# Chosen tokens' rows moved by indirect DMA instead of one-hot products, in an attention layer with a routed feed-forward

## The chip, the cores and the metric

The kernel runs on one core of a Trainium2 chip. The metric is the device time of one execution in microseconds. The profile and the trace are those of one execution; times in it count from its first instruction.

## What is computed

x has 8 batches of 512 tokens with 512 features, all fp32. Two layers follow each other, each with a residual sum:

```
x = x + attention(layernorm(x), Wq, Wk, Wv, Wg, Wo)      # 16 heads of 128, three kinds of attention, gated
z = layernorm(x);  w = z @ W_r + b_r                       # one routing weight a token
top 128 tokens by w are looked at; a token is chosen if w > the 128th value   (127 of 512 a batch)
x = x + (gelu(z[chosen] @ W1 + b1) @ W2 + b2) * w[chosen]  # chosen tokens; 2048 hidden features
x = x + z                                                  # the others
```

The change concerns the second layer only. It has a routing part, which finds each batch's chosen tokens and packs their rows of z into 128 slots (one stays empty), and an experts' part, two dense products over 8 x 128 slots, whose result goes back to the tokens' own rows.

## The kernel before

Up to about 1816 us of the trace the attention layer is computed; the change doesn't touch it. It leaves the heads' output in DRAM (o_scratch).

**Precision.** A product in fp32 is made from three fp32r products: each operand is split in a high half (a rounded copy, made by ScalarE) and a low half (value minus high half, by VectorE or GpSimd), and high times high, high times low and low times high are added in one bank.

**project_and_route (L1019).** For each batch the heads' output is multiplied by Wo. The 16 heads come in K = 4 chunks of G = 4. A chunk of batch b+1 is loaded by SyncE (load_o, 1 MB) into one of two raw buffers, ScalarE makes the high half (high, L1129), GpSimd the low half (chunks.low, L1015), and TensorE multiplies (chunk, L1191): 48 matmuls for all four blocks of 128 tokens. The routing of batch b is placed between the chunks of batch b+1, in an order written out by hand: in `body(b)` TensorE runs chunk 0 and chunk 1, then one product that spreads the routing weights as a row (L1210), chunk 2, two tiny products that give each chosen token its slot (L1218, L1219), half of chunk 3, then the packing (L1227 and L1231), then the other half of chunk 3.

VectorE adds x and the product (x1, L1264), takes mean and variance, makes z2 (L1288), the weights (L1295), counts how many weights are at least each token's (L1308), marks chosen tokens (sel), adds z of those not chosen (L1325), makes onehot (L1333: token against slot) and adds b2 times the weight (L1339). x1 is then the base of the output and SyncE stores it in base_scratch (L1108). As x1 is one buffer, L1264 of the next batch waits until this store has landed (base_stored), and row block t of the next batch's chunk 0 waits until L1264 has read bank t.

Packing a batch: 16 fp32 products of z2 with onehot (L1227, 32 passes in the trace) give z of the 128 slots, transposed; ScalarE and VectorE split it into zsel_hi and zsel_lo (L1149, L1342). Four transposes of onehot (L1231) give `place`, kept for later.

SyncE issues all transfers from one queue, in the order of its program. In `body(b)`: chunk 1 of batch b+1, x of batch b+1, chunk 2, chunk 3, chunk 0 of batch b+2, each behind the wait that frees its buffer, then the store of x1. At the start of the stage `load_first` (L995, L998) loads Wo's chunks and the first batch's chunks through the two raw buffers; the next Wo chunk waits until VectorE has made the low half of the one before (chunks.low_wo, L1010). Four small loads follow the first pair (L1113 to L1116).

**experts (L1354).** Two groups of 4 batches, 16 steps each, one per 128 hidden features. A step is `hidden` (L1551, 12 matmuls of the packed z with W1) for the step after, then 12 matmuls (L1589) of gelu's result with W2, accumulated in banks 0 to 3. The weights come by SyncE (L1424, L1425), their low halves by GpSimd (L1486). The first six steps of group 0 run inside the last batch's routing, where TensorE has no chunks left.

When a group is done its four banks are split (L1524, L1622) and `spread` (L1564, two matmuls for each of 4 blocks a batch) multiplies them by `place`, which puts the 128 slots back on 512 rows. VectorE multiplies by the weight and adds base (L1630); base comes back from DRAM (load_base, L1434) and goes to the output (L1439). For group 0 this happens one block a step during group 1, for group 1 at the end.

The loops over batches and over the steps of group 0 are loops of the engines (Fori).

## Time and profile before

| what | value |
|---|---|
| time, 3 runs | 2433.12, 2435.80, 2437.37 us; median 2435.8 |
| the profiled execution's own time | 2433.43 us |
| its span, first to last instruction | 2431.6 us |
| TensorE, VectorE, ScalarE, GpSimd busy | 2350.1, 1913.1, 1521.4, 1588.7 us |
| mean granted TensorE clock | 0.991 of 2.4 GHz |
| routing and projection | about 1816 to 2209 us |
| last batch's routing with the first expert steps | 2209 to 2262 us |
| experts after it | 2262 to 2431.6 us |

A row of the chain of waits has the start and the length of a piece, both in us, and the engine and line that worked or was waited for; it goes back from the last instruction through whatever released each step. A timeline row has the same two numbers, an instruction with its shapes and count, and in square brackets the idle time before it with what ended it. PE is TensorE, DVE VectorE, ACT ScalarE, POOL GpSimd, SPq the queue of SyncE.

### The profile page before, as it was taken

What the parts mean: (1) busy time and instruction counts of PE and PEld (TensorE: products, weight loads), DVE (VectorE), ACT (ScalarE), POOL (GpSimd) and SP (SyncE); (2) the same over time, 40 slices, a digit from 0 to 9 for tenths busy, and PEclk for the clock granted to TensorE, in tenths of its full rate; (3) what the DMA queues carried; (4) which work ended last, traced back from release to release, by engine and by line L of the source; (5) the groups of instructions that cost most, each with busy time, mean ns of one, the idle gap of its engine ahead of it and who ended that gap; (6) DMA issues with size and microseconds to landing.
All of it is one profiled execution on the core that took longest, in us unless ns stands there. A gap on an engine that the chain in (4) does not pass through costs nothing. (4 is left out here: it accounts for less than half of the span.)

```text
span 2431.6 us, 42771 instructions
## 1 busy us (share of the span) xinstructions
PE 2350.1 (97%) x13456; PEld 2067.5 (85%) x13456; DVE 1913.1 (79%) x6101; ACT 1521.4 (63%) x4192; POOL 1588.7 (65%) x1206
## 2 busy tenths in 40 slices
PE   6899999999999999999999999999969999999998
PEld 5799899989888998998999898889967888887776
DVE  7489898988888898988889888889864777775223
ACT  7577777777777777777777777777753222213442
POOL 1677877787787778778777877877744333433442
PEclk9999999999999999999999999999989999999999
DMA  5212222232222222222212222222225334332266
GB/s 169 73 53 66 72 75 62 66 83 55 66 72 75 54 74 78 60 62 76 75 53 75 76 62 60 78 56 63 62 99 187 121 103 154 139 104 87 97 184 221
DMA packets 143214, 215.44 MB, mean 89 GB/s; under 512 B 15136, under 2 KB 53408, under 8 KB 141984
## 3 DMA queue, kind: packets, MB, share of 16 engines
q1 hardware_dynamic: 143008, 212.95, 29.5%
q8 instruction: 99, 1.62, 0.3%
q14 instruction: 107, 0.88, 0.1%
HBM read 94.66 MB, written 51.12 MB: 60 GB/s over the span
## 5 line engine op out<-in xcount | busy, mean ns | idle before, releaser
L555 POOL TENSOR_TENSOR s_full<-s_full,rope 128x512 f32<-128x512 f32 x256 | 334.8, 1308 | 340.3 <-DMA s_swap<-s_full 340.0
L559 POOL TENSOR_TENSOR s_full<-s_full,s_swap 128x512 f32<-128x512 f32 x256 | 331.3, 1294 | 36.7
L556 POOL TENSOR_TENSOR s_swap<-s_swap,rope 128x512 f32<-128x512 f32 x256 | 331.2, 1294 | 0.0
L563 POOL TENSOR_TENSOR qk_lo<-s_full,qk_hi 128x512 fp32r<-128x512 f32 x256 | 326.5, 1296 | 0.0
L718 ACT ACTIVATE pt_hi<-bank 128x384 fp32r<-128x384 f32 (+1 forms) x384 | 174.9, 528 | 221.4 <-PE bank L657 221.0
L1015 POOL TENSOR_TENSOR o_lo<-o_raw,o_hi 128x2048 fp32r<-128x2048 f32 x32 | 149.6, 4675 | 241.7 <-ACT o_hi L1129 202.1
L613 PE MATMUL bank<-wv_hi,xt_hi 128*128 128x256 f32 x1024 | 300.2, 293 | 0.0
L724 ACT ACTIVATE bank<-bank,shift 128x512 f32<-128x512 f32 (+3 forms) x512 | 256.7, 501 | 58.9 <-DVE bank L829 58.3
L613 PE MATMUL bank<-wv_hi,xt_lo 128*128 128x256 f32 x1024 | 289.9, 283 | 0.0
L613 PE MATMUL bank<-wv_lo,xt_hi 128*128 128x256 f32 x1024 | 289.8, 283 | 0.0
L829 DVE TENSOR_REDUCE bank<-bank 128x8 f32<-128x512 f32 (+3 forms) x512 | 253.1, 494 | 0.0
L825 DVE TENSOR_REDUCE shift<-bank 128x1 f32<-128x512 f32 (+3 forms) x512 | 246.4, 481 | 0.0
L847 DVE SCALAR_TENSOR_TENSOR bank<-bank,coef,cb 128x192 f32<-128x192 f32 (+1 forms) x512 | 195.5, 405 | 50.4 <-ACT probs L743 50.3
L730 ACT ACTIVATE win<-win,shift 128x192 f32<-128x192 f32 (+1 forms) x512 | 225.5, 440 | 0.0
L713 ACT ACTIVATE qk_hi<-s_full 128x512 fp32r<-128x512 f32 x256 | 161.3, 630 | 83.5 <-POOL s_full L559 78.7
L600 PE MATMUL bank<-xt_hi,wq_hi 128*128 128x512 f32 x512 | 208.5, 407 | 3.4 <-PEq L193 3.4
L1191 PE MATMUL bank<-wo_hi,o_hi 128*128 128x512 f32 x512 | 204.6, 400 | 5.8 <-PEq L463 3.3
L839 DVE TENSOR_TENSOR pt_lo<-bank,pt_hi 128x384 fp32r<-128x384 f32 (+1 forms) x384 | 207.0, 595 | 1.1 <-ACT pt_hi L718 1.1
L600 PE MATMUL bank<-xt_hi,wq_lo 128*128 128x512 f32 x512 | 200.9, 392 | 0.0
L1191 PE MATMUL bank<-wo_hi,o_lo 128*128 128x512 f32 x512 | 200.0, 391 | 0.0
L1191 PE MATMUL bank<-wo_lo,o_hi 128*128 128x512 f32 x512 | 199.8, 390 | 0.0
L600 PE MATMUL bank<-xt_lo,wq_hi 128*128 128x512 f32 x512 | 199.4, 389 | 0.0
(181 smaller groups left out, 7028.3 us busy)
## 6 DMA issues: line engine op xcount, KB each, us to landing
s_swap<-s_full SPq DMA_DIRECT2D x512, 128.0 KB, 2.3
o_scratch<-s_swap SPq DMA_DIRECT2D x128, 256.0 KB, 2.0
o_raw<-o_scratch SPq DMA_DIRECT2D x32, 1024.0 KB, 6.2
w_raw<-in_L_ffn_W SPq DMA_DIRECT2D x64, 256.0 KB, 3.0
xin<-in_L_attn_x SPq DMA_DIRECT2D x14, 1024.0 KB, 5.6
base_scratch<-x SPq DMA_DIRECT2D x8, 1024.0 KB, 4.7
base<-base_scratch SPq DMA_DIRECT2D x32, 256.0 KB, 4.3
out<-base SPq DMA_DIRECT2D x32, 256.0 KB, 3.6
```

The lines of the kernel that those rows point to most:

```text
L555: nc.gpsimd.tensor_tensor(s_full[k][:], s_full[k][:], rope[:, 0, :], ALU.mult).then_inc(cos_done[k], 1)
L556: nc.gpsimd.tensor_tensor(s_swap[k][:], s_swap[k][:], rope[:, 1, :], ALU.mult).then_inc(sin_done[k], 1)
L559: nc.gpsimd.tensor_tensor(s_full[k][:], s_full[k][:], s_swap[k][:], ALU.add).then_inc(roped[k], 1)
L563: nc.gpsimd.tensor_tensor(qk_lo[k][:], s_full[k][:], f32(qk_hi[k][:]), ALU.subtract).then_inc(lo_done[k], 1)
L600: last = nc.tensor.matmul(banks[QK_BANK[k]][:, :], w[k][s][:, c, :], v[:, b, c, :], start=(n == 0), stop=(n == 3 * C - 1))
L613: last = nc.tensor.matmul(out, x[:, b, c, at:at + P], w[:, c, :], start=(n == 0), stop=(n == 3 * C - 1), skip_group_check=True)
L724: nc.scalar.activation(n, n, ACT.Exp, bias=shift1[:, t:t + 1], scale=-1.0, accum_out=sums[:, 1, t:t + 1]).then_inc(exp_row, 1)
L730: nc.scalar.activation(win[:, t, lo:], win[:, t, lo:], ACT.Exp, bias=shift2[:, t:t + 1], scale=-1.0, accum_out=sums[:, 2, t:t + 1]).then_i ...
L825: nc.vector.tensor_reduce(shift1[:, t:t + 1], n[:, 0:(t + 1) * P], AX.X, ALU.min)
L829: nc.vector.reduce_sum(sc[:, t, 0:nb], n[:, 0:nb * BS].rearrange("p (n s) -> p n s", s=BS), AX.X).then_inc(row_read, 1)
L839: nc.vector.tensor_tensor(pt_lo[:, PTOFF[g]:PTOFF[g] + w], banks[PT_BANK[g]][:, 0:w], f32(pt_hi[:, PTOFF[g]:PTOFF[g] + w]), ALU.subtract). ...
L1191: last = nc.tensor.matmul(banks[t][:, :], o[k % 2][:, g, t * P:(t + 1) * P], w[:, k * G + g, :], start=(k == 0 and n == 0), stop=(k == K - ...
```

## The change

Routing no longer packs rows by products. `store_z` writes z2 of a batch to DRAM (1 MB, rows of 2 KB); four tiny products of onehot with `tags` (a token's number and weight) give each slot its token (`info`); GpSimd turns that into row addresses and fetches the 128 rows by indirect DMA (`fetch_z`); in the next batch TensorE transposes them (`turn_rows`, four transposes) and ScalarE and VectorE split them (`z_high`, `z_low`). x1 is stored straight in the output, by rows of 2 KB. In the experts' part `fetch` gets the 128 rows of a batch from the output by indirect DMA, `final` adds the result times the weight in one instruction a batch, and `put_back` writes them to the output by indirect DMA; `place`, `spread`, the split of the results, load_base and store are gone. For the last batch the packing lies in group 0 behind step 11 (TURN). The loops over batches, over GpSimd's chunks and over group 0's steps are written out.

```diff
+    late = np.concatenate([before, slot, ones, p[:, None] - FAR], 1)
...
+    z_rows = r("z_rows", [P, D])
+    row_at, away = r("row_at", [P, B, 2], mybir.dt.int32), r("away", [P, B, 2])
+    z_dram = [nc.dram_tensor(f"z_scratch{b}", [N, D], F32, kind="Internal").ap() for b in range(B)]
+    tags = r("tags", [P, T, 2])
     G, K, wo_hi, wo_lo = chunks.G, chunks.K, chunks.wo_hi, chunks.wo_lo
...
         eng.wait_ge(chunk_used, B * K + 1)
+    def fetch_z(pool, b):
+        pool.wait_ge(info_done, b + 1)
+        for i, start in enumerate((0, b * N)):
+            nc.gpsimd.tensor_scalar(away[:, b, i:i + 1], info[:, b, 0:1], float(FAR + start), None, ALU.add).then_inc(rows_addressed, 1)
+        pool.wait_ge(rows_addressed, 3 * b + 2)
+        nc.gpsimd.tensor_copy(row_at[:, b], away[:, b]).then_inc(rows_addressed, 1)
+        pool.wait_ge(rows_addressed, 3 * b + 3)
+        pool.wait_ge(z2_stored, 16 * (b + 1))
+        if b:
+            pool.wait_ge(zsel_ready, b)
+        nc.gpsimd.indirect_dma_start(z_rows[:], None, z_dram[b], bass.IndirectOffsetOnAxis(ap=row_at[:, b, 0:1], axis=0),
+                                     bounds_check=N - 1, oob_is_err=False).then_inc(z_rows_loaded, 16)
+    def turn_rows(pe, b):
+        pe.wait_ge(z_rows_loaded, 16 * (b + 1))
+        if b:
+            pe.wait_ge(zsel_lo_done, b)
+        for c in range(C):
+            last = nc.tensor.transpose(banks[7][:, c * P:(c + 1) * P], z_rows[:, c * P:(c + 1) * P], m("ident"))
+        last.then_inc(zsel_ready, 1)
+    def z_high(act, b):
+        act.wait_ge(zsel_ready, b + 1)
+        nc.scalar.activation(zsel_hi[:, :, b * P:(b + 1) * P], banks[7][:, :].rearrange("p (c s) -> p c s", c=C), ACT.Copy)\
+            .then_inc(zsel_hi_done, 1)
+    def z_low(dve, b):
+        dve.wait_ge(zsel_hi_done, b + 1)
+        nc.vector.tensor_tensor(zsel_lo[:, :, b * P:(b + 1) * P], banks[7][:, :].rearrange("p (c s) -> p c s", c=C),
+                                f32(zsel_hi[:, :, b * P:(b + 1) * P]), ALU.subtract).then_inc(zsel_lo_done, 1)
     ex_sync, ex_gpsimd, ex_scalar, ex_tensor, ex_vector = experts(
-        nc, at, chunks, r, banks, zsel_hi, zsel_lo, place, weight, base_dram,
-        (wait_used, wait_raw_free, wait_split_free, zsel_lo_done, place_done, base_stored), w1, b1, w2, b2, out)
+        nc, at, chunks, r, banks, zsel_hi, zsel_lo, info, row_at, (fetch_z, turn_rows, z_high, z_low),
...
+            def store_z(b):
+                sp.wait_ge(z2_ready, b * T + T)
...
                 if more:
                         load_o(b + 1, k)
                         if k == 1:
                             load_x(b + 1)
+                            store_z(b)
                     if more != "next":
                         load_o(b + 2, 0)
                 else:
                     for f in range(EARLY + 2):
                         first(f)
+                        if f == 3:
+                            store_z(b)
                 sp.wait_ge(base_ready, b * T + T)
-                sp.dma_start(base_dram[bass.ds(b, 1)].rearrange("o p t d -> p (o t) d"), x1[:]).then_inc(base_stored, 16)
+                sp.dma_start(out[b].rearrange("(t p) d -> p t d", p=P), x1[:]).then_inc(base_stored, 16)
...
                 act.wait_ge(step, b * NS + 9)
                 nc.scalar.activation(sd[:], ve[:], ACT.Sqrt).then_inc(sd_ready, 1)
+                if b:
+                    z_high(act, b - 1)
...
-                act.wait_ge(zsel_ready, b + 1)
-                nc.scalar.activation(zsel_hi[:, :, bass.ds(b * P, P)], banks[6][:, :].rearrange("p (c s) -> p c s", c=C),
-                                     ACT.Copy).then_inc(zsel_hi_done, 1)
-                act.wait_ge(place_ready, b + 1)
-                nc.scalar.activation(place[:, bass.ds(b, 1), :], banks[7][:, :], ACT.Copy).then_inc(place_done, 1)
+                act.wait_ge(info_ready, b + 1)
+                nc.scalar.activation(info[:, b, :], banks[6][:, 0:2], ACT.Copy).then_inc(info_done, 1)
...
                 chunks.low(pool, 0, k, 1)
-            with pool.Fori(0, B - 1) as b:
-                for k in range(K):
+            nc.gpsimd.memset(z_rows[:], 0.0).then_inc(rows_cleared, 1)
+            pool.wait_ge(rows_cleared, 1)
+            chunks.low(pool, 1, 0, 0)
+            for b in range(B - 1):
+                for k in range(1, K):
                     chunks.low(pool, b + 1, k, k % 2)
+                if b < B - 2:
+                    chunks.low(pool, b + 2, 0, 0)
+                fetch_z(pool, b)
             first, rest = ex_gpsimd(pool)
...
                 if more:
                     chunk(b + 1, 0)
+                    if b:
+                        turn_rows(pe, b - 1)
...
                 else:
                     first(5)
                 pe.wait_ge(onehot_ready, b * T + T)
-                for c in range(C):
-                    for t in range(T):
-                        last = nc.tensor.matmul(banks[6][:, c * P:(c + 1) * P], z2[:, t, c * P:(c + 1) * P], onehot[:, t, :],
-                                                start=(t == 0), stop=(t == T - 1))
-                last.then_inc(zsel_ready, 1)
                 for t in range(T):
-                    last = nc.tensor.transpose(banks[7][:, t * P:(t + 1) * P], onehot[:, t, :], m("ident"))
-                last.then_inc(place_ready, 1)
+                    last = nc.tensor.matmul(banks[6][:, 0:2], onehot[:, t, :], tags[:, t, :], start=(t == 0), stop=(t == T - 1))
+                last.then_inc(info_ready, 1)
...
                 after()
+                if b:
+                    dve.wait_ge(z2_stored, 16 * b)
                 for t in range(T):
...
-                did(v.tensor_scalar(weight[:, bass.ds(b, 1), :], wraw[:].rearrange("p (o t) -> p o t", o=1), br_all[:, 0:1], None, ALU.add))
+                if b:
+                    dve.wait_ge(info_done, b)
+                else:
+                    dve.wait_ge(tags_set, 1 + T)
+                did(v.tensor_scalar(tags[:, :, 1], wraw[:], br_all[:, 0:1], None, ALU.add))
                 after()
                 for t in range(T):
                     v.tensor_scalar(diag[:, t * P:(t + 1) * P], m("ident"), wcol[:, t:t + 1], None, ALU.mult).then_inc(diag_ready, 1)
+                if b:
+                    z_low(dve, b - 1)
                 if not more:
                     first(2)
                 dve.wait_ge(row_ready, b + 1)
...
-                dve.wait_ge(zsel_hi_done, b + 1)
-                v.tensor_tensor(zsel_lo[:, :, bass.ds(b * P, P)], banks[6][:, :].rearrange("p (c s) -> p c s", c=C),
-                                f32(zsel_hi[:, :, bass.ds(b * P, P)]), ALU.subtract).then_inc(zsel_lo_done, 1)
                 assert at[0] == NS, (at[0], NS)
             v.memset(selcum[:], 0.0)
+            v.memset(tags[:], 0.0).then_inc(tags_set, 1)
+            dve.wait_ge(tags_set, 1)
+            dve.wait_ge(small_loaded, 64)
+            for t in range(T):
+                v.tensor_scalar(tags[:, t, 0:1], number, float(t * P), None, ALU.add).then_inc(tags_set, 1)
             for k in range(1, K):
                 chunks.low_wo(dve, k)
             first, rest = ex_vector(dve)
...
-        if g:
-            for f in range(FT):
-                body(g * FT // 2 + f // 2, f % 2, f, f == 0, f == FT - 1)
-            return
-        with eng.Fori(begun // 2, FT // 2 - 1) as pair:
-            for s in range(2):
-                body(pair, s, pair * 2 + s, False, False)
-        for s in range(2):
-            body(FT // 2 - 1, s, FT - 2 + s, False, s == 1)
+        for f in range(0 if g else begun, FT):
+            body(g * FT // 2 + f // 2, f % 2, f, f == 0, f == FT - 1)
...
+            tiles(sp, 1, load)
+            sp.wait_ge(base_stored, 16 * (B + 1))
+            sp.wait_ge(rows_stored, 16 * B)
...
+        def fetch(b):
+            pool.wait_ge(rows_cleared, 1)
+            pool.wait_ge(base_stored, 16 * (b + 2))
+            nc.gpsimd.indirect_dma_start(rows[:, b, :], None, out_rows, bass.IndirectOffsetOnAxis(ap=row_at[:, b, 1:2], axis=0),
+                                         bounds_check=B * N - 1, oob_is_err=False).then_inc(rows_loaded[b], 16)
+        def put_back(b):
+            pool.wait_ge(final_ready, b + 1)
+            nc.gpsimd.indirect_dma_start(out_rows, bass.IndirectOffsetOnAxis(ap=row_at[:, b, 1:2], axis=0), rows[:, b, :], None,
+                                         bounds_check=B * N - 1, oob_is_err=False).then_inc(rows_stored, 16)
+        def low_and_rows(pair, s, f, first, last):
+            low(pair, s, f, first, last)
+            g = pair // (FT // 2)
+            if not g and f == EARLY + 1:
+                fetch_z(pool, B - 1)
+            if 8 <= f < 8 + GB:
+                fetch(g * GB + f - 8)
+            if g and 2 <= f < 2 + GB:
+                put_back(f - 2)
         def rest():
             for g in range(NG):
-                tiles(pool, g, low)
+                tiles(pool, g, low_and_rows)
+            for q in range(GB):
+                put_back(GB + q)
...
+        def body_and_z(pair, s, f, first, last):
+            body(pair, s, f, first, last)
+            if f == TURN:
+                z_high(act, B - 1)
...
-                    pe.wait_ge(ff_lo_done, (g - 1) * GB + q + 1)
+                    pe.wait_ge(final_ready, (g - 1) * GB + q + 1)
...
-                if both and q:
-                    if q == GB - 1:
-                        ins.then_inc(step_done, 1)
-                    for t in range(T):
-                        spread(g * GB + q - 1, t)
-            if not both:
-                ins.then_inc(step_done, 1)
+            ins.then_inc(step_done, 1)
+        def step_and_z(pair, s, f, first, last):
+            step(0, pair, s, f, first, last)
+            if f == TURN:
+                turn_rows(pe, B - 1)
...
+        def final(b):
+            g, q = divmod(b, GB)
+            dve.wait_ge(rows_loaded[b], 16)
+            if q < GB - 1:
+                dve.wait_ge(ffacc_ready, g * (GB - 1) + q + 1)
+            else:
+                dve.wait_ge(step_done, FT if g < NG - 1 else NG * FT - 1)
+            nc.vector.scalar_tensor_tensor(out=rows[:, b, :], in0=banks[q][:, :], scalar=info[:, b, 1:2], in1=rows[:, b, :],
+                                           op0=ALU.mult, op1=ALU.add).then_inc(final_ready, 1)
         def low_and_final(pair, s, f, first, last):
             low(pair, s, f, first, last)
             if first:
                 for q in range(GB):
-                    low_rows(0, q)
-            for n in range(f - 1 if f else 0, f + 1 if last else f):
-                final(n // T, n % T)
+                    final(q)
+        def low_and_z(pair, s, f, first, last):
+            low(pair, s, f, first, last)
+            if f == TURN:
+                z_low(dve, B - 1)
         def rest():
-            tiles(dve, 0, low)
+            wait_used(dve)
+            nc.vector.memset(rows[:], 0.0).then_inc(rows_cleared, 1)
+            tiles(dve, 0, low_and_z)
             tiles(dve, 1, low_and_final)
-            low_rows(1, 0)
             for q in range(GB):
-                if q + 1 < GB:
-                    low_rows(1, q + 1)
-                for t in range(T):
-                    final(GB + q, t)
+                final(GB + q)
         return lambda f: early(f, low), rest
```

Gone with it, and not shown: split_rows and low_rows (the split of the results), spread and its calls, load_base, store and load_and_store on SyncE.

## Rows read from the trace of the kernel before

**Rows 1.** The chain of waits around one batch's routing (start, length, what ended last).
```profile
2095.26 5.60 PE bank L1191 x24
2100.85 3.57 PE bank L1227 x32
2104.43 0.44 PE bank L1231 x4
2104.86 27.22 PE bank L1191 x120
...
2132.94 10.92 PE bank L1191 x48
...
2143.98 0.22 PE bank L1219 x2
```

**Rows 2.** Timeline of VectorE in that batch (start, length, line, operation).
```profile
2108.61 2.48 DVE L1264 TENSOR_TENSOR x<-xin,bank 128x512 f32<-128x512 f32 x4 [2.60 <-DMA base_scratch<-x]
...
2119.72 1.92 DVE L1288 TENSOR_SCALAR z<-x,mv,y 128x512 f32<-128x512 f32 x4
...
2145.47 7.06 DVE L1339 SCALAR_TENSOR_TENSOR x<-b_all,wsel,x 128x512 f32<-128x512 f32 x4
```

**Rows 3.** Timeline of GpSimd: two of the low halves of a chunk.
```profile
2123.23 4.94 POOL L1015 TENSOR_TENSOR o_lo<-o_raw,o_hi 128x2048 fp32r<-128x2048 f32 x1 [4.16 <-ACT o_hi L1129]
...
2145.89 4.77 POOL L1015 TENSOR_TENSOR o_lo<-o_raw,o_hi 128x2048 fp32r<-128x2048 f32 x1 [7.18 <-ACT o_hi L1129]
```

**Rows 4.** Timeline of SyncE: the transfers it issues in that batch (start, issue time).
```profile
2103.75 0.37 SPq L1108 DMA_DIRECT2D base_scratch<-x  x1
2104.67 0.37 SPq L1089 DMA_DIRECT2D o_raw<-o_scratch  x1
...
2111.81 16.90 SPq L1089 DMA_DIRECT2D o_raw<-o_scratch  x3
```

**Rows 5.** DMA issues in 2103 to 2105 us (KB each, us to landing).
```profile
base_scratch<-x SPq DMA_DIRECT2D x1, 1024.0 KB, 4.7
o_raw<-o_scratch SPq DMA_DIRECT2D x1, 1024.0 KB, 6.4
```

**Rows 6.** Tile o_raw, 1900 to 2210 us: landing of its transfers.
```profile
DMA to landing us min/median/max: 4.6/6.4/8.9
```

**Rows 7.** Timeline of ScalarE: the high half of the chunk after it.
```profile
2121.23 1.92 ACT L1129 ACTIVATE o_hi<-o_raw 128x2048 fp32r<-128x2048 f32 x1 [5.32 <-PE bank L1191]
```

**Rows 8.** The chain of waits in the last batch.
```profile
2228.98 4.57 PE bank L1589 x12
...
2255.74 3.59 PE bank L1227 x32
...
2262.35 2.99 PE bank L1551 x12
```

**Rows 9.** Timeline of SyncE at the start of the stage.
```profile
1819.56 0.44 SPq L1116 DMA_DIRECT2D br_all<-in_L_ffn_b_r  x1
1826.21 0.38 SPq L995 DMA_DIRECT2D o_raw<-in_L_attn_Wo  x1
```

**Rows 10.** DMA issues at 1819.4 to 1820 us.
```profile
br_all<-in_L_ffn_b_r SPq DMA_DIRECT2D x1, 0.5 KB, 7.6
```

**Rows 11.** The chain of waits at the start of the stage.
```profile
1827.14 4.56 POOL o_lo L1015
...
1831.72 4.66 DMA o_raw<-o_scratch
```

**Rows 12.** The chain of waits in the experts' second group and at the end.
```profile
2322.46 2.76 PE bank L1551 x12
2325.23 0.47 PE bank L1564 x2
...
2405.22 2.73 PE bank L1551 x12
...
2410.20 1.64 PE bank L1589 x6
```

114 lines of the change are left out of this document (23 added, 91 removed).

## The prediction

> **What bounds the kernel now.** I read the chain of waits first, around one batch of the routing. From 2095.26 to 2144.20 us it is TensorE alone, without a gap [rows 1]: half of chunk 3 (5.60), the packing products (3.57), onehot's transposes (0.44), the other half of chunk 3 with chunks 0 and 1 of the next batch (27.22), chunk 2 (10.92), the slot products. The period is 48.94 us. Call 2095.26, where the slots are known, S. The timelines of the other engines then show how near each is to becoming the bound, since the change takes work from TensorE and gives the others new waits. In the experts' second group the chain alternates between TensorE and late weights; at the end it runs through ScalarE, VectorE and stores.
>
> Three figures of that batch decide the forecast. TensorE ends chunk 3 at 2104.86 + 5.46 = 2110.32, while VectorE frees bank 0 for chunk 0 at 2108.61 + 0.62 = 2109.23 [rows 2]; VectorE had waited there for the store of x1, issued at 2103.75 [rows 4]. So the lead is only 1.1 us. z is complete at 2119.72 + 1.92 = 2121.64 [rows 2]. And the load of chunk 2 is issued at 2111.81 or just after [rows 4], some 21 us before TensorE wants it at 2132.94.
>
> **Routing, TensorE's side.** Gone are 3.57 and 0.44 us a batch, new are 8 passes of the tiny products at 0.11 (two take 0.22 [rows 1]), so 0.89, and four transposes, 0.44. Ahead of chunk 0 TensorE gains 3.57 + 0.44 - 0.89 = 3.12 us, but x1 is late next: bank 0 is free at 2109.23 and not sooner, because the store of x1 still has to land. Of 3.12 us some 1.1 are left, and the transposes take 0.44 of these back. The store now writes 2 KB rows; I leave its landing at 4.7 us [rows 5].
>
> **Routing, the queue of SyncE.** `store_z(b)` stands behind the load of x and ahead of the load of chunk 2. It waits for z, so chunk 2 and chunk 3, which were issued at once when their buffers were free, now wait for z too. With z at 2121.64 the store is issued at about 2121.75 and chunk 2 right behind it, ten microseconds later than before. How long does the second of two such megabytes take? The pair of x1's store and chunk 1 shows it: issued at 2103.75 and 2104.67, the second lands 6.4 later [rows 4, 5], 7.3 after the first issue. The longest landing of this tile is 8.9 [rows 6], which gives 9.4; the shortest is 4.6. I take 8.0, somewhat over the pair, since chunk 3 is now queued right behind. Landed at 2129.75, the chunk needs ScalarE and GpSimd: from 2121.23 [rows 7] to 2123.23 + 4.94 = 2128.17 [rows 3], 6.94 us. It is ready at 2136.7. TensorE, started at 2109.23, wants it 22.62 + 0.44 us later, at 2132.3, and waits 4.4. Then 10.92 and 0.34 to the next S: 2147.95 in place of 2144.20, **+3.75 us a batch**. The period is now a closed chain: x1 stored, z, z stored, chunk 2 loaded, split, multiplied.
>
> A wait also costs clock. Behind a short wait in the last batch 12 matmuls took 4.57 us [rows 8] where 12 take 2.73 at 10.92 for 48 [rows 1]: 1.84 us more, most of it at 1.2 in place of 2.4 GHz. Some waits will be followed by this and some not; I take half, +0.9. Six periods follow the first S: 6 x 4.65 = +27.9. In the first batch no store of x1 precedes z, which is ready about 1.5 us earlier in relation to TensorE: +2.1 (1.4 to 4). Behind the last S of these nothing waits for a store, so TensorE's 3.12 are gained: -3.1.
>
> The fetch itself costs nothing as long as it is covered. GpSimd ends the low half of the next batch's chunk 0 at S + 6.5 [rows 3] and gets the next piece when chunk 1 has landed (2111.07) and ScalarE has taken 1.92 over it, at S + 17.7: 11.2 us in which three small instructions and one indirect DMA must fit, and `turn_rows` asks for the rows only at S + 25. No row shows an indirect DMA. Its bounds on GpSimd are nothing and 4.94, its longest instruction here; either fits. If the cover is gone, each microsecond above it is added to every batch.
>
> GpSimd and VectorE get in each other's way: L1339's four pieces took 7.06 us in place of about 2.5 (0.62 each, as L1264) while GpSimd's 4.77 us ran [rows 2, 3]. That is VectorE waiting for GpSimd. The Trainium skill, "SBUF — State Buffer", section "A bandwidth-pool intuition that's wrong (but worth ruling out)", states the other direction too: a DMA issued from GpSimd waits for its descriptors while VectorE holds the shared port, some 3.1 us in place of 0.6. By that rule the sum would stay as it is, as long as 11.2 us of room hold it; the case in which they don't is a rival below.
>
> **Start of the stage.** VectorE now fills `tags` before its first `low_wo`, and for that waits for all four small loads. The last is issued at 1819.56 [rows 9] and lands 7.6 later [rows 10], at 1827.16. GpSimd begins its chunk at 1827.14 and holds to 1831.70 [rows 11], and VectorE is held with it, as in L1339. The 2048-wide subtraction (4 x 0.62) then ends at about 1834.2 in place of 1826.2, when SyncE was released for the next Wo chunk [rows 9]. That chunk and the heads' chunk, before issued at 1831.72 and landed 4.66 later [rows 11], now go as a pair: 1834.2 + 8.0 = 1842.2 in place of 1836.4. **+5.8**, and TensorE has no work to hide it. If VectorE isn't held, +2.
>
> **Last batch.** ScalarE's `z_high` stands between the root and the next expert step and waits for transposes that follow a whole step on TensorE (2.73); `z_low` adds 0.62 to VectorE, on which this stretch hangs: +2.8 (0.6 to 3.4). The packing: from 2255.74 to 2262.35 [rows 8] are 6.61 us, products, ScalarE, GpSimd; new are 0.89 for the products and about 2.2 of the 3.0 behind them, as a 512-wide copy turns into a tiny one: -3.5. Behind step 11 the transposes: +0.4.
>
> **Experts.** In the second group a step has its 24 matmuls at 2.73 for 12, a pair of `spread` (0.47) and late weights, which wait on SyncE behind stores. From 2322.46 to 2405.22 + 2.73 = 2407.95 [rows 12] are 85.5 us; 27 twelves at 2.72 are 73.4. With spread, load_base and store gone, **-12.1**. GpSimd has two 512-wide low halves a step, an estimate of 2 x 4.56 / 4 = 2.3 us from [rows 11], in 5.4 us; a fetch of up to 3 us hides there too.
>
> **End.** From 2407.95 to the span's end at 2431.6 are 23.65. New: 2.25 until the last product starts (2410.20), 24 matmuls at 0.23, so 5.5, `final` 0.76, then `put_back`. I take 1.5 us on GpSimd (bounds 0 and 4.94) and 3.3 to landing (bounds 0 and 4.7, a megabyte's store): 13.3, so **-10.3** (-6 to -15). The Trainium skill, "DMA: Bandwidth & Descriptors", section "Anatomy of one DMA — SWDGE (gpsimd) path", gives 2.0 us plus bytes over 436 GB/s, 2.6 us for 256 KB; by it the end would be some 2 us shorter. No run here shows that yet.
>
> **Sum.** +5.8 + 2.1 + 27.9 - 3.1 + 2.8 - 3.5 + 0.4 - 12.1 - 10.3 = +10.0 on the profiled execution's 2433.4. The median of the three runs is 2.4 above that, so the forecast is 2435.8 + 10 = **2446 us**. Own range, with landing and clock at their ends: 2430 to 2464.
>
> **Rivals.** First, *the second load isn't late* (not slower, faster): if a store and a load run beside each other and chunk 2 lands 4.6 us after its own issue, the lowest of [rows 6], it is ready at 2133.7, the wait is 1.4, the clock holds, and a period costs +0.8. With the first batch at nothing the sum is -15: **2421 us**. It decides below a landing of about 6 us. Against it speaks the pair in [rows 5], for it that 4.6 occurs. Chance 0.17.
>
> Second, *TensorE's saving shows in full*: eight times 3.57 + 0.44 - 0.89 - 0.44 = 2.68 is 21.4, with 3 behind the last packing and 12.1 and 10.3 from the experts: -47, **2389 us**. The 1.1 us of lead of x1 in [rows 2] speak against it, and the place of the store in the queue. Chance 0.05.
>
> Third, *costs and gains cancel*: the second landing is 7.3 as in the pair, the clock is mostly kept, the start costs 2 to 6: between -4 and +4, **2436 us**. Chance 0.16.
>
> Fourth, *the fetch holds GpSimd beyond its 11.2 us*, since VectorE keeps it from writing its list of rows (the skill's rule above). At 16 us of GpSimd a batch all of chunk 1's low half, and z behind it, is 5 us later: +30 more, **2476 us**. For it speaks only that the two engines do hold each other up; against it that VectorE is idle from S + 8.4 to S + 13.4. Chance 0.10.
>
> **Numbers.** The forecast has 0.52, of which 0.02 lie within the bound below. A measurement of this kernel tells 0.2% from no change, 4.9 us: faster is below 2430.9, slower above 2440.7. Faster: 0.17 + 0.05 = 0.22. Same: 0.16 + 0.02 = 0.18. Slower: 0.50 + 0.10 = 0.60. The range is 2420 to 2464: it takes in the first and third rival and leaves out the second and fourth, 0.15, and a little at the edges.
>
> **What the changed profile would show.** Right: S to S is 52 to 54 us; ahead of chunk 2 TensorE waits 3 to 5 us for GpSimd's L1015 and that for the landing of o_raw; ahead of chunk 0 it waits about 2 us for L1264, that for the store of x1; chunk 3 of batch 0 starts some 6 us late; the second group is a closed row of twelves at 2.72. Wrong: a gapless chain of TensorE in the routing with a period under 49 (first or second rival), or TensorE waiting for z_rows or for GpSimd behind a fetch (fourth).

## The result, and the profile after

The changed kernel takes 2451.35 us (median of 4 runs, 2449.86 to 2454.69), the kernel before beside it on the same chip 2434.46 us (4 runs, 2431.48 to 2437.37): ratio 1.0062, 95% interval 1.0049 to 1.0074, slower by 15 us by the ratio (12 to 18), by 16.9 between the two medians. The forecast was 2446 us. The profiled execution is the longest of its four: it took 2454.69 us with a span of 2452.8, against 2433.43 and 2431.6 before, so the two traces are 21.2 us apart, 4 more than the medians. The first page, part 1, and the issues of part 6 that are new or have moved:

```profile
PE 2332.6 (95%) x13200; PEld 2046.6 (83%) x13200; DVE 1882.6 (77%) x6075; ACT 1500.4 (61%) x4173; POOL 1623.4 (66%) x1255
...
o_raw<-o_scratch SPq DMA_DIRECT2D x32, 1024.0 KB, 7.6
...
z_scratch<-z SPq DMA_DIRECT2D x8, 1024.0 KB, 5.5
out<-x SPq DMA_DIRECT2D x8, 1024.0 KB, 5.3
```

I went through the trace stage by stage, cutting both at the same instruction. S is the start of VectorE's copy of the slots, 0.04 us behind the prediction's S; "six periods" are the six stretches from one S to the next:

| stretch | forecast | measured | after |
|---|---|---|---|
| up to the stage (unchanged code) | 0 | +2.1 | starts at 1818.70 |
| start of the stage, to batch 0's last product | +5.8 | +7.9 | |
| first batch, to the first S | +2.1 | +3.7 | S at 1913.16 |
| six periods | +27.9 | +27.7 | 52.62, 55.62, 51.98, 55.35, 52.01, 53.76 |
| last of these S to the first expert product | -3.1 | +0.5 | 2234.50 to 2250.86 |
| last batch | +2.8 | +0.6 | |
| packing to the next hidden product | -3.5 | -3.7 | 2298.23 to 2301.14 |
| rest of the experts' first group | +0.4 | +4.5 | 2301.14 to 2365.78 |
| second group | -12.1 | -12.0 | 2365.78 to 2439.23 |
| end | -10.3 | -10.1 | 2439.23 to 2452.8 |
| sum | +10.0 | +21.2 | |

Where before TensorE had no wait at all in six periods of 48.95 us, it now has two in each. The list of waits of TensorE from 1905 to 2236 us (engine, line, what it waited for: total, times, longest):

```profile
PE bank L1241 <- DVE x L1312: 15.4, 6, 2.8
PE bank L1241 <- POOL o_lo L1016: 12.4, 6, 3.1
```

The first is for x1 ahead of chunk 0, the second for the low half of chunk 2. One period, from S at 2073.38, shows where each comes from. VectorE, SyncE, ScalarE, GpSimd and TensorE, each from its timeline (start, length, line, operation; in brackets the idle time before it and what ended it); they answer to [rows 2], [rows 4], [rows 7] and [rows 3]:

```profile
2074.61 7.07 DVE L1395 SCALAR_TENSOR_TENSOR x<-b_all,wsel,x 128x512 f32<-128x512 f32 x4
2087.25 2.48 DVE L1312 TENSOR_TENSOR x<-xin,bank 128x512 f32<-128x512 f32 x4 [5.57 <-issue]
...
2097.75 1.92 DVE L1338 TENSOR_SCALAR z<-x,mv,y 128x512 f32<-128x512 f32 x4
```

```profile
2081.71 0.38 SPq L1153 DMA_DIRECT2D out<-x  x1
...
2099.69 0.36 SPq L1136 DMA_DIRECT2D z_scratch<-z  x1
2100.09 15.87 SPq L1127 DMA_DIRECT2D o_raw<-o_scratch  x3
```

```profile
2109.04 1.92 ACT L1174 ACTIVATE o_hi<-o_raw 128x2048 fp32r<-128x2048 f32 x1 [7.12 <-DMA o_raw<-o_scratch]
```

```profile
2075.10 4.71 POOL L1016 TENSOR_TENSOR o_lo<-o_raw,o_hi 128x2048 fp32r<-128x2048 f32 x1 [8.52 <-ACT o_hi L1174]
2080.02 1.07 POOL L1088 TENSOR_SCALAR away<-info 128x1 f32<-128x1 f32 x2 [0.21 <-ACT info L1196]
...
2082.50 1.11 POOL L1095 DMA_INDIRECT z_rows<-z_scratch,row_at  x1 [0.77 <-POOL row_at L1090]
```

```profile
2088.09 0.68 PE L1241 MATMUL bank<-wo_hi,o_hi 128*128 128x512 f32 x1 [2.75 <-DVE x L1312]
...
2115.63 0.80 PE L1241 MATMUL bank<-wo_hi,o_hi 128*128 128x512 f32 x1 [2.55 <-POOL o_lo L1016]
```

Read it backwards. TensorE waits at 2115.63 for GpSimd, GpSimd waited for ScalarE, and ScalarE at 2109.04 for o_raw, whose load was issued at 2100.09, right behind z's store, which had waited for z. That is the queue of the forecast. The other wait, at 2088.09, goes back to x1's four adds at 2087.25, these to the store of x1 issued at 2081.71, and that to the four pieces of L1395, which took 7.07 us beside GpSimd's low half of 4.71.

The end is as long as forecast. GpSimd's timeline there has the four indirect stores one behind another, the first released by VectorE's last sum of batch 4:

```profile
2444.79 1.02 POOL L1505 DMA_INDIRECT out<-rows,row_at  x1 [6.19 <-DVE rows L1630]
2446.17 0.98 POOL L1505 DMA_INDIRECT out<-rows,row_at  x1 [0.36 <-issue]
2447.49 0.97 POOL L1505 DMA_INDIRECT out<-rows,row_at  x1 [0.34 <-issue]
2448.85 0.97 POOL L1505 DMA_INDIRECT out<-rows,row_at  x1 [0.39 <-issue]
```

### The profile page after: what moved, and what is told of

Read it like the earlier page. It is cut to its first block and busy times, and to the rows that moved or that the text cites. A ratio compares the mean times of both kernels' runs of the same rounds, so it can differ in the third digit from the quotient of the medians.

```text
span 2452.8 us, 41653 instructions
## 1 busy us (share of the span) xinstructions
PE 2332.6 (95%) x13200; PEld 2046.6 (83%) x13200; DVE 1882.6 (77%) x6075; ACT 1500.4 (61%) x4173; POOL 1623.4 (66%) x1255
## 5 line engine op out<-in xcount | busy, mean ns | idle before, releaser
L1241 PE MATMUL bank<-wo_hi,o_hi 128*128 128x512 f32 x512 | 211.2, 412 | 40.6 <-POOL o_lo L1016 17.6
L1241 PE MATMUL bank<-wo_lo,o_hi 128*128 128x512 f32 x512 | 206.5, 403 | 0.0
L1241 PE MATMUL bank<-wo_hi,o_lo 128*128 128x512 f32 x512 | 206.3, 403 | 0.0
```

The lines of the kernel that those rows point to most:

```text
L1241: last = nc.tensor.matmul(banks[t][:, :], o[k % 2][:, g, t * P:(t + 1) * P], w[:, k * G + g, :], start=(k == 0 and n == 0), stop=(k == K - ...
```

## Experiments: which part costs what

Twelve kernels, in the order of what they ask. The kernel before, run beside each group, had medians of 2436.3 to 2437.3 us, up to 3 more than beside the changed kernel (2434.46), so a difference of 3 us between the medians of two groups says little by itself. All edits are against the changed kernel unless said.

**The new experts' part alone.** Routing packs by products, as before; the addresses are still made (from the same small products), but z is neither stored nor fetched.

```
-        nc.gpsimd.indirect_dma_start(z_rows[:], None, z_dram[b], bass.IndirectOffsetOnAxis(ap=row_at[:, b, 0:1], axis=0),
-                                     bounds_check=N - 1, oob_is_err=False).then_inc(z_rows_loaded, 16)
...
-                            store_z(b)
...
-                        turn_rows(pe, b - 1)
...
+                for c in range(C):
+                    for t in range(T):
+                        last = nc.tensor.matmul(banks[7][:, c * P:(c + 1) * P], z2[:, t, c * P:(c + 1) * P], onehot[:, t, :],
+                                                start=(t == 0), stop=(t == T - 1))
+                last.then_inc(zsel_ready, 1)
```

> The experts' part of the change with the old packing: z is packed by the 16 products again, without the store of z, the fetch of its rows and their transposes; tags, info and the row addresses stay, onehot's transposes don't come back. Theory: the routing is a gapless chain of TensorE again, at 48.94 - 0.44 + 0.80 = 49.3 us a batch; the start keeps its 7.9 us, the experts give back their 22: 2434.5 + 6 x 0.4 + 8 + 2 - 22, some 2425 (2420 to 2430). Rival (the written-out loops or x1's store by 2 KB rows are what slows the routing): the period stays above 51 us and the time above 2436.

Measured: 2423.32 us (ratio 0.9950, 0.9932 to 0.9968), six periods of 49.46 to 49.47 us. This part is worth 13.6 us, as the theory said, net of what it still carries: the tags at the start (the first S comes 5.4 us later behind the stage's first load than in the kernel before) and 0.5 us more in each period. The rest, z by way of DRAM, therefore costs 28 us net, against 2451.35. Written-out loops and x1's store in rows of 2 KB slow nothing in the six periods: TensorE has no wait there.

**The place of z's store in SyncE's queue.** First behind the load of chunk 2; then only the wait for z ahead of chunk 2, and the store itself behind chunk 3.

```
                         if k == 1:
                             load_x(b + 1)
-                            store_z(b)
+                        if k == 2:
+                            store_z(b)
```

```
                         if k == 1:
                             load_x(b + 1)
-                            store_z(b)
+                            sp.wait_ge(z2_ready, b * T + T)
+                        if k == 3:
+                            store_z(b)
```

> The store of z is issued behind the load of chunk 2 instead of ahead of it; all else, the extra megabyte a batch too, stays. Theory (its place in the queue makes the load of chunk 2 wait for z): the wait of TensorE ahead of chunk 2, up to 5.2 us, is gone; what is left is the wait for x1's store ahead of chunk 0, so a period of 53.6 us falls to 48.5 to 50.3, the first batch loses its 3.6 too, and the time falls by 23 to 34 us from 2451, to 2417 to 2428. Rival (the added traffic itself, or the written-out loops, cost the time): less than 5 us of it comes back.

> SyncE still waits for z ahead of the load of chunk 2, but the store of z goes out only behind the load of chunk 3. It parts the wait from the megabyte that stands ahead. Theory: both count, as chunk 2 lands 9.3 us after z in the changed kernel; alone it lands 5 to 6.5 us after, so a period falls by about 3 us and the time by 15 to 20 us, to about 2433. Rival 1 (only the wait counts, transfers run beside each other): within 5 us of 2451. Rival 2 (only the megabyte ahead counts): as low as with the store moved whole, under 2428.

Measured: 2426.5 us (0.9953, 0.9935 to 0.9972) and 2418.77 us (0.9923, 0.9906 to 0.9939). The same number of bytes, and chunk 2 is on time in all six periods of the first: it was the place, not the traffic. Not all of the gain is the place's. Its six periods take 291.4 us in place of 321.3; of these 29.9 us, 12.4 are the waits for chunk 2, 4.9 are waits for x1 that two periods no longer have, and the rest is the same products at a higher clock. The second run splits it further. SyncE's wait alone, with no megabyte behind it, leaves chunk 2 late by 0.4 us in one period of six. So of the two things that `store_z` put ahead of chunk 2, the wait for z and the megabyte, the megabyte decides: the run's second rival held. (z was early in four of these periods; but in the forced order below, with z just as early and the megabyte ahead, all six wait for chunk 2, and with z late here, at S + 26, they wait 0.4 and nothing.) What is left of waits in the two kernels, 1905 to 2195 us, z_later first:

```profile
PE bank L1242 <- DVE x L1313: 10.5, 4, 2.9
```

```profile
PE bank L1243 <- DVE x L1314: 5.0, 2, 2.6
PE bank L1243 <- POOL o_lo L1016: 0.4, 1, 0.4
```

Four and two of six periods still wait for x1. The others don't wait at all and last 46.38 us. Periods of two kinds in one execution of one program asked for a cause of their own.

**Which of VectorE and GpSimd is held.** In periods of 46.38 the pieces of L1395 had taken 2.74 us and GpSimd's low half 6.70; in the others 7.07 and 4.71. One period of the kernel with the tags last, VectorE and GpSimd:

```profile
2014.43 2.74 DVE L1395 SCALAR_TENSOR_TENSOR x<-b_all,wsel,x 128x512 f32<-128x512 f32 x4
```

```profile
2014.91 6.70 POOL L1016 TENSOR_TENSOR o_lo<-o_raw,o_hi 128x2048 fp32r<-128x2048 f32 x1 [10.33 <-ACT o_hi L1174]
```

GpSimd starts 0.48 us behind VectorE here and 0.49 behind in the period shown above, yet here GpSimd is the one held. What decides between the two I can't read from the program, and no run shows it. The kernel before and the changed one fell the slow way in all of their profiled periods. One wait takes the choice away, as GpSimd then starts only when VectorE is done:

```
                 if b < B - 2:
+                    pool.wait_ge(base_ready, b * T + T)
                     chunks.low(pool, b + 2, 0, 0)
```

> The changed kernel with one wait added: GpSimd's low half for chunk 0 of the batch after next waits for VectorE's four writes of b2 times weight into x1 (they started 0.5 us apart, and one held the other: the four writes took 7.1 us, or 2.7 us and then the low half took 6.7 us). Theory: which of the two is held is decided by their order alone, so with the order fixed the writes take 2.7 us in all six periods, x1's store is issued 4.0 us behind the slots' copy instead of 8.3, TensorE waits for no x1 ahead of chunk 0, and the periods are those of 48.0 to 51.0 us that the tags-last kernel's profile showed with the short writes (mean 49.4), 296.6 us for six instead of 321.3: about 2427 us. Rival 1: the order does not decide, the writes stay at 7 us: 2451 us. Rival 2: GpSimd's low half comes late instead (it ends at about 8.7 us behind the copy) and pushes chunk 0 and all behind it by 2 us a period: about 2440 us.

Measured: 2427.05 us (0.9965, 0.9952 to 0.9978), six periods that sum to 296.7 us (48.06, 50.98, 47.94, 51.08, 50.67, 47.97). What the theory needs is shown: VectorE's four pieces take 2.74 us and x1's store goes out at S + 4.0 in all six, and the wait for x1 is gone from TensorE's list:

```profile
PE bank L1242 <- POOL o_lo L1016: 12.1, 6, 2.8
```

One added wait gives 24 us, as much as moving the store. Alone, the later store gives periods of 48.6 us in the mean and the forced order 49.5; both are needed for 46.38 in every period.

**x1 in two buffers.** The other way to free the adds of the store.

```
-    x1 = r("x1", [P, T, D])
+    x1s = [r(f"x1_{k}", [P, T, D]) for k in range(2)]
...
-                dve.wait_ge(base_stored, b * 16 + 16)
+                if b >= 2:
+                    dve.wait_ge(base_stored, b * 16)
```

> x1 gets two buffers, so that x1 of a batch no longer waits for the store of the one before; the store of z stays ahead of chunk 2. Theory (z, its store and chunk 2 close the chain, and z itself is held by chunk 1's low half, not by x1): TensorE starts chunk 0 about 2.6 us earlier and waits that much longer ahead of chunk 2; the time changes by 0 to -6 us. Rival (the wait for x1's store adds to the period): 2.6 us a batch, 15 us less.

Measured: 2443.91 us (1.0028, 1.0010 to 1.0046), 10 runs from 2435.13 to 2454.24. It fell between theory and rival. In the profiled execution the first add stood at S + 3.9 in four periods and at 8.2 in two, the same two outcomes; at 8.2 z was begun no earlier than S + 23.4 and TensorE waited 4.7 us for chunk 2, where it waited 1.3 to 2.8 in the other four. The buffer doesn't cure the hold; it only moves where it bites.

**The tags at the start.**

```
-            v.memset(tags[:], 0.0).then_inc(tags_set, 1)
-            dve.wait_ge(tags_set, 1)
-            dve.wait_ge(small_loaded, 64)
-            for t in range(T):
-                v.tensor_scalar(tags[:, t, 0:1], number, float(t * P), None, ALU.add).then_inc(tags_set, 1)
             for k in range(1, K):
                 chunks.low_wo(dve, k)
+            v.memset(tags[:], 0.0).then_inc(tags_set, 1)
+            dve.wait_ge(tags_set, 1)
+            dve.wait_ge(small_loaded, 64)
+            for t in range(T):
+                v.tensor_scalar(tags[:, t, 0:1], number, float(t * P), None, ALU.add).then_inc(tags_set, 1)
```

> VectorE fills tags behind the three low halves of Wo, not ahead of them. Theory: the start of the stage is as in the kernel before again; the change had cost 7.9 us there, two of them lower clock, so the time falls by 6 to 8 us, to about 2444. Rival (the delay of the start comes from elsewhere, for instance the fetch of instructions of the written-out loops): no change beyond 2 us.

Measured: 2431.83 us (0.9983, 0.9968 to 0.9998), 10 runs from 2427.33 to 2442.76, 19.5 under the changed kernel. That is more than twice what theory gave, so not all of it is the tags. From the stage's first load to the first S are 94.46 us in the changed kernel (1818.70 to 1913.16) and 85.25 here (1820.93 to 1906.18), 9.2 us apart. Each is one trace, though: of the other kernels that are the same as the changed one up to there, some took 95.7 and 95.8 us (the shifted halves, the doubled fetch), some 90.3 (the forced order, the moved fetch). So the tags cost between 5.0 and 10.6 us, and what makes the difference is not shown. The rest is luck in the order above: four of six periods fell the short way (48.0 to 51.0 us). The start in the changed kernel, on VectorE:

```profile
1828.97 0.34 DVE L1404 TENSOR_SCALAR tags<-late 128x1 f32<-128x1 f32 x4 [10.10 <-DMA br_all<-in_L_ffn_b_r]
1829.22 6.38 DVE L1011 TENSOR_TENSOR wo_lo<-o_raw,wo_hi 128x2048 fp32r<-128x2048 f32 x1
```

The tags themselves are 0.34 us. What they cost is that the subtraction now meets GpSimd's low half (1828.90, 4.55 us) and takes 6.38 us, where it takes 2.29 alone:

```profile
1828.39 2.29 DVE L1011 TENSOR_TENSOR wo_lo<-o_raw,wo_hi 128x2048 fp32r<-128x2048 f32 x1 [7.33 <-ACT wo_hi L1003]
```

That row is of the kernel with the tags last.

**Is the fetch covered?** Each of the first six fetches of z's rows is issued twice, the second into a tile that nobody reads.

```
+        if b < B - 2:
+            if b:
+                pool.wait_ge(more_loaded, 16 * b)
+            nc.gpsimd.indirect_dma_start(z_more[:], None, z_dram[b], bass.IndirectOffsetOnAxis(ap=row_at[:, b, 0:1], axis=0),
+                                         bounds_check=N - 1, oob_is_err=False).then_inc(more_loaded, 16)
```

> Each of the first six batches' rows of z is fetched twice, the second time into a tile that nobody reads. Theory (the fetch is covered: GpSimd has some 10 us of idle time there and the rows are asked for late): 6 x 1.9 us of more work of GpSimd costs under 2 us in all. Rival (the fetch is on the path of each batch, as descriptors or as traffic): 1 us or more a batch, 6 us or more.

Measured: 2451.8 us (1.0060, 1.0044 to 1.0077) against 2451.35, periods 321.3 us in sum as without. GpSimd spends 1.11 us on a fetch in the timeline and 1.00 on the second; even doubled it is free in the six periods.

**The end of the routing and the experts' first group.** Two orders. The fetch for batch 6 behind the first low halves of the experts and that for batch 7 a step later; and ScalarE's and VectorE's halves of the last packed batch one step behind the transposes.

```
                 if b < B - 2:
                     chunks.low(pool, b + 2, 0, 0)
-                fetch_z(pool, b)
+                    fetch_z(pool, b)
             first, rest = ex_gpsimd(pool)
             for f in range(EARLY):
                 first(f)
+                if f == 0:
+                    fetch_z(pool, B - 2)
...
-            if not g and f == EARLY + 1:
+            if not g and f == EARLY + 2:
                 fetch_z(pool, B - 1)
```

```
-            if f == TURN:
+            if f == TURN + 1:
                 z_high(act, B - 1)
...
-            if f == TURN:
+            if f == TURN + 1:
                 z_low(dve, B - 1)
```

> GpSimd's fetch for the last batch but one goes behind the first expert step's low halves, and the fetch for the last batch one step later. Theory (behind these fetches stand low halves for which TensorE has nothing to do): TensorE's wait of 4.4 us before the first expert product falls by about 2.7 us (three small instructions, the descriptors and the gaps between), and the one after the last packing by up to 2.7: 3 to 5 us less than 2451. Rival (those waits are for the weights' landing alone): no change.

> ScalarE and VectorE split the last batch's packed rows one step later than TensorE transposes them. Theory: ScalarE no longer waits for the transposes ahead of the next weights' high half, TensorE's stop behind step 11 shrinks from 3.0 us to the transposes' 0.45: 2.5 us less. Rival: the stop stays and the time with it.

Measured: 2457.34 us (1.0087, 1.0070 to 1.0104) for the first, a miss: the fetch for batch 6 was out of the way of the first expert product, whose wait fell from 4.40 to 1.16 us, but stood ahead of the second step's low halves, and a wait of 2.2 us came back there. List of waits, 2220 to 2400 us, this kernel and the changed one:

```profile
PE bank L1575 <- POOL w_lo L1497: 14.0, 6, 3.4
```

```profile
PE bank L1573 <- POOL w_lo L1495: 12.5, 5, 4.4
```

The other fetch did the harm. One step later is step 8, where GpSimd also begins to fetch the experts' rows, so that two indirect DMAs now stand ahead of the same low halves. GpSimd's timeline:

```profile
2301.68 1.11 POOL L1095 DMA_INDIRECT z_rows<-z_scratch,row_at  x1 [0.93 <-POOL row_at L1090]
2304.34 0.99 POOL L1502 DMA_INDIRECT rows<-out,row_at  x1 [1.55 <-issue]
2305.35 2.52 POOL L1497 TENSOR_TENSOR w_lo<-w_raw,w_hi 128x512 fp32r<-128x512 f32 x2
```

TensorE waits 3.44 us for these, where the changed kernel waits 0.92, and the rest of the first group is 4.1 us longer than there. From the last S to the second group the trace is 2.9 us longer in all. Its span of 2449.5 is 3 us under the changed kernel's only by what lies ahead of that S, where the program is the same; its three other executions took 2457.2 to 2459.9 us.

The second gave 2448.77 us (1.0044, 1.0026 to 1.0061), 2.6 less than the changed kernel. The two intervals overlap, but the trace shows the gain in its place: the rest of the first group is 2.75 us shorter. Its chain behind step 11 runs without a gap:

```profile
2329.74 2.72 PE bank L1595 x12
2332.46 0.44 PE bank L1103 x4
2332.90 2.77 PE bank L1573 x12
```

In the changed kernel it goes through ScalarE and GpSimd there:

```profile
2335.30 0.45 PE bank L1103 x4
...
2335.80 0.47 issue
2336.27 0.63 ACT w_hi L1533
...
2336.97 1.27 POOL w_lo L1495
...
2338.29 3.01 PE bank L1573 x12
```

**All that helped, together.** z's store behind chunk 3, the forced order, the tags last, the halves a step later; then the same with x1 in two buffers.

> The changed kernel with four edits: the wait of the run before; z stored behind the load of chunk 3; the tags made behind the low halves of Wo; the last batch's high and low halves of z one step later. Theory: no wait of TensorE is left in the six periods, 46.38 us each (the value that both kernels with z stored later show where x1 is early), 278.3 us instead of 321.3; 6.9 us at the start of the stage and 2.6 us behind step 11: 2451.4 - 43.0 - 6.9 - 2.6 = 2399 us, below both kernels. Rival: z's store at a quarter of a period later makes GpSimd's fetch and with it the transposes of the next batch late, and TensorE waits for the rows by about 1 us a period: about 2405 us.

> The run before with x1 in two buffers as well. Theory: with the order fixed TensorE waits for no x1, so a second buffer gives nothing: the time of the run before, within 3 us. Rival: the batch norm's chain starts 5 us earlier and takes VectorE out of the way of GpSimd's low half of chunk 1; any wait left in the periods goes and the time is some 5 us under the run before.

Measured: 2403.05 us (2396.9 to 2406.25; 0.9854, 0.9842 to 0.9867) and 2399.04 us (2397.71 to 2404.4; 0.9853, 0.9839 to 0.9867). Both beat the kernel before by 33 us or more. The first is 4 us over its theory of 2399. The theory's six periods came out to the hundredth, 46.38 or 46.39 each; the windows view over them (1903.00 to 2181.20: length, then busy time and count of TensorE, its weight loads, VectorE, ScalarE, GpSimd, granted clock, DMA share, GB/s), and over the six of the changed kernel:

```profile
1903.00:2181.20 278.20, 278.20 (x1261) 228.80 (x1261) 199.83 (x391) 50.81 (x42) 121.23 (x48) 1.00 0.47 161
```

```profile
1913.20:2234.50 321.30, 293.50 (x1261) 236.74 (x1261) 206.24 (x390) 51.49 (x42) 126.82 (x48) 0.96 0.41 139
```

The same 1261 matmuls: 43.1 us apart, of which 27.8 are waits and 15.3 are the granted clock. The second buffer gave nothing that the intervals can tell, with the wait for x1 gone.

**One more edit, for what the forecast had missed behind the last S.** ScalarE copied the info of batch 6 only behind its first high half of W1, and so GpSimd's addresses and fetch came late, between that half and its own low half. In the changed kernel's chain:

```profile
2246.00 0.61 ACT w_hi L1533
2246.76 0.22 POOL away L1088
...
2248.30 1.11 POOL z_rows L1095
2249.44 1.28 POOL w_lo L1495
2250.86 7.85 PE bank L1573 x24
```

```
-                    if more == "next":
-                        first(-1)
...
                 nc.scalar.activation(info[:, b, :], banks[6][:, 0:2], ACT.Copy).then_inc(info_done, 1)
+                if more == "next":
+                    first(-1)
```

> The kernel with four edits (2403.05 us) with one more: ScalarE copies the info of the last batch but one out of PSUM ahead of the first high halves of W1 and W2, not behind them. In the changed kernel's trace GpSimd made that batch's addresses only at 2246.76 us, 0.15 us behind the first high half of 0.61 us, and its addresses and fetch (2246.76 to 2249.41, 2.65 us) stood in the chain between ScalarE's high half and the first low half. Theory: the copy alone was late, by its place in ScalarE's program; moved, the fetch runs while W1 and W2 load, the first low half follows the high half at once, and TensorE's wait ahead of the first expert product falls by 2.65 us: about 2400.4 us. Rival: as in the run in which the fetch was moved behind the first low half, what is won there is lost at the next low halves, which wait for TensorE's products all the same: 2403 us.

Measured: 2395.15 us (2391.16 to 2400.56; 0.9834, 0.9821 to 0.9848), 7.9 under the kernel without the edit, where theory had 2.65. The chain of this kernel now has the low half directly behind the high half:

```profile
2188.52 0.64 ACT w_hi L1535
2189.24 1.29 POOL w_lo L1497
...
2190.66 5.70 PE bank L1575 x24
```

TensorE's wait there fell from 4.44 to 1.18 us, and behind the shorter wait 24 products took 5.70 us where they had taken 8.61. These two, 3.3 and 2.9, make 6.2 us. Between the last S and the next the two traces are 10.9 us apart (63.19 and 52.27), and not all of that need be the edit's: from the first expert product to the next S the kernel without it took 46.8 us, as two others did (46.4 with the order forced, 46.7 with z's store behind chunk 2), while seven kernels took 40.8 to 41.6, the changed one among them. What parts these two groups I have not found. This is the best version: 41 us under the kernel before, 56 under the changed one.

## Why the prediction was right, and where its steps were off

**The cause and the sign hold.** The step that carried the forecast, that `store_z` ahead of chunk 2 makes that chunk late, is shown twice over by moving it. Its times hold as well: z's store was forecast at S + 26.5 and went out at 25.9 to 26.3; the second megabyte was forecast 8.0 behind it and landed 7.8 to 9.3 behind it; chunk 2 was to be ready at S + 41.4 and TensorE began it at 40.4 to 42.2.

**The split of a period was off, and that its sum was not is luck.** Against 46.38 us without a wait, the six periods have 4.6 us of waits each and 2.5 of clock; I had 6.4 of waits (2.0 for x1, 4.4 for chunk 2) and 0.9 of clock. The two errors cancel. "Some waits will be followed by this and some not; I take half" held as a share: the lower clock follows seven of the twelve waits. But I charged it once a period, at half of 1.84 us, where a period has two waits, and each of the seven costs 2.2 us (15.3 in all). It explains why periods alternate between 52 and 55 us: with the clock low behind the wait for x1, products on the way to chunk 2 are slower, and chunk 2's wait is shorter by as much; low behind chunk 2, nothing hides it. The windows view of five us behind each wait has a granted clock of 0.53 to 0.70 for the seven, mixes of the two levels of 1.2 and 2.4 GHz, and of 1.00 for the other five. Four of the twelve, behind waits for x1 (1980, 2088) and for chunk 2 (2006, 2115):

```profile
1980.00:1985.00 5.00, 4.53 (x20) 3.81 (x21) 4.92 (x14) 1.92 (x1) 1.07 (x1) 1.00 0.69 235
2006.00:2011.00 5.00, 4.02 (x10) 3.14 (x11) 4.93 (x5) 0.00 (x0) 5.00 (x2) 0.53 0.55 200
...
2088.00:2093.00 5.00, 4.92 (x15) 3.91 (x16) 4.92 (x13) 1.91 (x1) 1.17 (x1) 0.66 0.70 232
2115.00:2120.00 5.00, 4.37 (x12) 3.50 (x13) 4.93 (x5) 0.00 (x0) 5.00 (x2) 0.66 0.56 210
```

**The wait for x1.** "Of 3.12 us some 1.1 are left" is near for this trace, a little high: TensorE waits 2.4 to 2.75 us for x1, so 0.4 to 0.7 are left. I took bank 0's time as given by the store. What made that store late was the 7.06 us of L1339 [rows 2], which I had read and put down to GpSimd, without asking what would follow if it took 2.7. That was the larger lever: 24 us by one wait. In the kernel before TensorE never waits for x1 in the six periods: its products hid the delay.

**The start** was 7.9 for 5.8. VectorE was held as forecast: its low half ended at 1835.60. The pair behind it landed later than my 8.0: ScalarE began on the heads' chunk at 1845.23, 9.2 us behind the issue of its own load at 1836.05. TensorE's waits of 4.3 and 3.4 us there also cost clock, for which I had nothing: up to batch 0's last product TensorE is busy for 48.97 us where it was 46.26, at a granted clock of 0.91 in place of 0.97. That is 2.7 of the 7.9 us.

**The step that failed** is "Behind the last S of these nothing waits for a store, so TensorE's 3.12 are gained: -3.1". It was +0.5. TensorE did reach the expert products 3.1 us earlier, 11.9 behind S in place of 15.0, but waited 4.40 us there where it had waited 0.78. Two things made that wait. GpSimd's address work and fetch, 2.65 us, stood between ScalarE's high half and its own low half. The rest is the weights: the load that ends last goes out 1.0 us behind x1's store and takes 5.92 us, and then the halves have to be made; with the fetch out of the way, in the last run, 1.18 us of wait are left. I had counted GpSimd's room only in the period, where it is covered, and not in the one place where `fetch_z` meets the experts. The last run shows what put it there: ScalarE's copy of the info.

**Behind step 11** I had the transposes alone, 0.4. The rest of the first group was 4.5 longer. Of these 3.0 stand behind step 11, the transposes and a wait of 2.55, as `z_high` waits for them on ScalarE, with the next high half of W2 queued behind it; 0.9 is a wait at 2307.81 behind the fetch for batch 7, which I had not counted; the last 0.6 are the twelve products behind each of the two waits, 3.01 us in place of 2.72. The shifted order took 2.75 of this away. It is the same oversight as in the last batch, where I did count ScalarE's wait, and too high: 2.8 for 0.6. First batch: 3.7 for 2.1, not taken apart further; with the tags last it and the start together are 9.2 us shorter in the one trace of that kernel.

**Experts and end**: -12.0 for -12.1 and 13.57 us for 13.3. The end's parts were not those of the forecast, though. I had one indirect store on the path, of 1.5 us and 3.3 to landing; there are four in a row, 1.32 to 1.38 us apart, of 0.97 to 1.02 us each, and 3.0 us from the last one's end (2449.82) to the end of the span. From the end of VectorE's last sum (2448.06) to the end of the span are 4.8 us, just the forecast's 1.5 and 3.3, but made of other parts: 0.8 until the fourth store begins behind the third, 0.97 on GpSimd, 3.0 to the end. That the sum holds is luck. The Trainium skill, "DMA: Bandwidth & Descriptors", section "Anatomy of one DMA — SWDGE (gpsimd) path", gives 2.0 us plus the bytes over 436 GB/s, an estimate of 2.6 us for the 256 KB of such a store. The trace of the version with four edits has their landing, 2.7 us behind their issue, which agrees.

**The rivals.** The first (the second load isn't late) and the second (the saving shows in full) are dead for the kernel as changed; but with the queue and the order mended, periods of 46.38 us are the second rival's forecast of 2.68 us saved (2.57 were). The third is dead too: the second megabyte lands 7.8 to 9.3 us behind the first's issue where this rival has 7.3, and the clock was not kept. The fourth fell with the doubled fetch. Its rule, the Trainium skill's "SBUF — State Buffer", section "A bandwidth-pool intuition that's wrong (but worth ruling out)", has descriptors wait while VectorE holds the shared port. No run here shows such a wait. In the version with four edits the fetch at 2005.83 lies beside VectorE's adds (from 2004.72) and still lands in 3.4 us, though whether these adds hold the port is not shown; in the changed kernel, with VectorE idle, the fetch at 2082.50 landed in 8.0, behind a store and a load of a megabyte each, issued 0.8 and 0.4 us earlier.

**Left open**: the 2.1 us ahead of the stage, in code that is the same. The stage's first load goes out anywhere between 1815.85 and 1821.71 in the fourteen traces, so 2.1 is no more than they differ among themselves. Open too is what decides which of VectorE and GpSimd is held, and what makes the start and the last batch 5 us longer in some kernels than in others that are the same there.

## What to carry to other kernels

A DMA that waits for data must not stand in a queue ahead of one that was free to go, and here its bytes counted for more than its wait: ask where in the queue the new transfer can stand, and take the last place its reader allows. Where two engines hold each other up, look at which of them the path needs, and make it go first with a wait; a hold that is hidden before a change is the first thing to show when the change takes the cover away. Work moved to another engine must be followed to the places where that engine is on the path, at the start and the end of loops above all, and with it whatever feeds it (here a copy of two columns on a third engine).

## What the runs showed of the hardware

- VectorE and GpSimd on SBUF tiles side by side: with starts 0.5 us apart either VectorE's 2.74 us become 7.07 and GpSimd takes 4.71, or VectorE keeps 2.74 and GpSimd takes 6.70. Both occur in one execution of one program. Even a write of 128x4 is held: L1321 at 2092.57 took 3.90 us and ended with GpSimd's low half of chunk 1, at 2096.4; the same instruction takes 0.17 (median of eight) in the kernel before.
- An indirect DMA of 128 rows of 2 KB takes GpSimd 1.11 us with 0.77 us ahead of it behind its addresses, and landed 7.6 to 8.1 us behind its issue in the six periods of the changed kernel, where two megabytes had been issued less than 1 us before, and in 3.4 to 3.6 in the version with four edits, where that was 5.6 us and more before.
- Of two transfers of a megabyte issued 0.4 us apart on SyncE's queue, the second lands 7.8 to 9.3 us behind the first one's issue in the six periods; at the start of the stage it landed 9.2 us behind its own issue.
- The same 1261 products of the six periods are busy for 15.3 us longer with twelve waits of 1.1 to 3.2 us among them than with none: behind seven of the twelve the granted clock is 0.53 to 0.70 over five us, behind five it is 1.00.
